# Expert places by half tiles of 64 tokens: 12 whole tiles, 7 pairs of halves and one half in place of 23 whole tiles

## The reference

```
logits = xf @ gate_w + gate_b                    # 2048 x 8
pb = softmax(logits);  top 1 of 8 experts per token
for each expert e:                               # scan
    h = gelu(xf @ w1[e] + b1[e])                 # 256 -> 1024
    y = h @ w2[e] + b2[e]                        # 1024 -> 256
    acc = acc + weight[:, e] * y                 # weight is 0 for the experts not chosen
x = x + acc
```

## Time and profile before

| | us |
|---|---|
| median of 3 runs | 841.37 |
| the profiled execution, whole time | 840.62 |
| its span, first to last instruction | 838.8 |
| TensorE busy in the span | 770.2 (92%) |
| VectorE, ScalarE, GpSimd busy | 442.7, 255.5, 186.9 |
| last stage: first tile's first product starts at | 661.4 |
| last scatter issued at | 832.4 |

### The profile page before, as it was taken

How to read it: one execution, slowest core, us unless ns; L and a number is a source line. 1 busy time by engine, 2 the same in 40 slices (tenths; PEclk the granted TensorE clock), 3 DMA queues, 4 the chain that set the end, 5 groups by cost and what they waited for, 6 DMA issues and landing times.

```text
span 838.8 us, 11312 instructions
## 1 busy us (share of the span) xinstructions
PE 770.2 (92%) x4207; PEld 625.8 (75%) x4207; DVE 442.7 (53%) x845; ACT 255.5 (30%) x502; POOL 186.9 (22%) x180
## 2 busy tenths in 40 slices
PE   5998999998989999999999999889886599999996
PEld 4665676687878878887888787645565599999995
DVE  3564678988922953295339532787966311111111
ACT  1533314222211221122122212455642223333331
POOL 3012353533000200020002000455631222222221
PEclk9999999999999999999999999979997699999999
DMA  9962600005000000000000000090122767776640
GB/s 327 385 201 88 264 0 2 1 0 202 2 1 2 2 3 2 2 2 2 2 2 2 2 2 3 8 394 1 51 76 76 255 221 219 227 214 218 205 137 0
DMA packets 20524, 79.68 MB, mean 95 GB/s; under 512 B 3053, under 2 KB 12400, under 8 KB 15664
## 3 DMA queue, kind: packets, MB, share of 16 engines
q1 hardware_dynamic: 17504, 70.44, 24.5%
q0 software_dynamic: 2944, 8.13, 2.5%
HBM read 72.27 MB, written 18.74 MB: 109 GB/s over the span
## 4 chain that ended last, share of the span: by engine, by line
PE 73%; DVE 18%; issue 5%; ACT 3%; DMA 1%; POOL 0%; DVEq 0%; SPq 0%; ACTq 0%; POOLq 0%
PE ps L1133 28%; PE ps L1824 10%; PE ps L1836 9%; PE ps L550 4%; PE ps L501 3%; PE ps L487 2%; DVE f_ha_hi L1233 2%; DVE f_raw L1227 2%; PE ps L1271 2%; DVE head_max L1661 1%; PE ps L579 1%; DVE stats L282 1%; PE ps L1408 1%; DVE c_tok L1662 1%; PE ps L1420 1%
## 5 line engine op out<-in xcount | busy, mean ns | idle before, releaser
L1210 ACT ACTIVATE f_raw<-ps,cols 128x512 f32<-128x512 f32 x96 | 66.2, 690 | 250.2 <-PE ps L1133 218.6
L1133 PE MATMUL ps<-f_hb_hi,fh 128*128 128x512 f32 x256 | 101.2, 395 | 2.5 <-DVE inexact L335 2.5
L1133 PE MATMUL ps<-f_ha_hi,fh 128*128 128x512 f32 x256 | 100.0, 391 | 3.2 <-ACT f_raw L1210 3.2
L1133 PE MATMUL ps<-f_hb_lo,fh 128*128 128x512 f32 x256 | 100.6, 393 | 0.0
L1133 PE MATMUL ps<-f_ha_lo,fh 128*128 128x512 f32 x256 | 99.6, 389 | 0.0
L1824 PEld LDWEIGHTS ps<-xsT,ew 128*128 128x128 f32 x736 | 87.2, 195 | 2.8 <-DVE xsT L1951 1.7
L1824 PE MATMUL ps<-xsT,ew 128*128 128x128 f32 x736 | 87.7, 278 | 1.1 <-DVE xsT L1951 1.1
L1884 ACT ACTIVATE hT<-ps,ew 128x128 f32<-128x128 f32 x184 | 52.5, 369 | 105.6 <-PE ps L1824 105.6
L1836 PE MATMUL ps<-ew,hT 128*128 x368 | 83.1, 379 | 0.0
L1233 DVE CAST f_ha_hi<-f_raw 128x512 fp32r<-128x512 f32 x64 | 32.8, 512 | 89.4 <-ACT f_raw L1210 88.3
L1836 PEld LDWEIGHTS ps<-ew,hT 128*128 128x128 f32 x368 | 68.2, 190 | 8.4
(11 more groups left out here) (241 smaller groups left out, 1290.0 us busy)
## 6 DMA issues: line engine op xcount, KB each, us to landing
ew<-in_ew SPq DMA_DIRECT2D x23, 1028.0 KB, 5.9
fh<-fh_copy SPq DMA_DIRECT2D x2, 4096.0 KB, 15.0
ew<-in_ew SPq DMA_DIRECT2D x1, 8192.0 KB, 23.4
fw<-fw_copy SPq DMA_DIRECT2D x3, 1024.0 KB, 7.1
eb<-in_eb SPq DMA_DIRECT2D x23, 128.0 KB, 3.3
x_res<-in_x SPq DMA_DIRECT2D x4, 512.0 KB, 10.8
rows<-x_res SPq DMA_DIRECT2D x4, 512.0 KB, 3.0
rows<-xn_e SPq DMA_DIRECT2D x4, 512.0 KB, 3.1
```

The source lines that it names most:

```text
L1133: ins = nc.tensor.matmul(out, *((xk, wk) if swap else (wk, xk)), start=(k == 0 and part == 0), stop=(k == w.shape[1] - 1 and part == 1))
L1210: nc.scalar.activation(f_raw[:, m % 3, :], ps[:, ring_bank(n), :], ACT.Silu if m < KH else ACT.Gelu, scale=col(("w1_s", "h1_s", "h2_s")[m ...
```

## The change

Places are given out by halves of 64 instead of tiles of 128. Each expert gets as many whole tiles as its number of halves allows (`g_first_i[:, 0]`, an even number of halves) and at most one odd half (`g_first_i[:, 1]`). The program has 12 tiles that belong to one expert each, 7 tiles that are pairs of halves with an expert of its own for each half, and one half alone: 20 tiles. They are worked in the order 0 to 3 whole, then a pair and a whole one by turns, then the last whole one and the half (`ORDER`). Loads of first weights become 27 in place of 23, in a ring of 6 buffers in place of 4.

For a pair, `up` makes 32 calls with 64 moving columns, 16 for each expert, and the gelu is 16 instructions of 64 columns. `down` makes 16 calls: for each k one with the 64 places of the first expert, which writes partitions 0 to 63, and one for the second expert, which writes partitions 64 to 127 (two column tiles of the array). The second one's weights are copied beforehand by VectorE from `ew2` to `ew2_b` (`second_weights`). At the head of the stage the one-hot tables grow from 23 to 40 columns and some small instructions are added.

```
-MT = NT + E - 1
+MT = NT + E // 2
+MH = 2 * MT
+FULL = NT - E // 2
+ORDER = [0, 1, 2, 3]
+for _n in range(FULL, MT - 1):
+    ORDER += [_n, len(ORDER) - (_n - FULL)]
+ORDER += [FULL - 1, MT - 1]
+HALVES = [2 if FULL <= _n < MT - 1 else 1 for _n in ORDER]
...
+LOAD_RING = 6
+PAIRED = [t for t in range(MT) if HALVES[t] == 2]
...
         def up(t):
-                for h in range(2):
+                loads = [(FIRST_LOAD[t] + h) for h in range(HALVES[t])]
...
                     for q in range(4):
-                        for k in range(KD):
-                            at_ = k * HID + (4 * h + q) * P
-                            ins = nc.tensor.matmul(ps[:, 2 + 2 * (t % 2) + h, q * P:(q + 1) * P],
-                                                   ew1[u][:, at_:at_ + P], xsT[:, t % 2, k, :],
-                                                   start=(k == 0), stop=(k == KD - 1))
+                        for h, n in enumerate(loads):
+                            part = slice(0, P) if t in WHOLE else half_rows(h)
+                            for k in range(KD):
+                                at_ = k * HID + (4 * g + q) * P
+                                ins = nc.tensor.matmul(
+                                    ps[:, 2 + 2 * (t % 2) + g, q * P + part.start:q * P + part.stop],
+                                    ew1[n % LOAD_RING][:, at_:at_ + P], xsT[:, t % 2, k, part],
+                                    start=(k == 0), stop=(k == KD - 1))
...
         def down(t):
+                if t in PAIRED:
+                    pe.wait_ge(e_w2, PAIRED.index(t) + 1)
...
-                    ins = nc.tensor.matmul(ps[:, 6 + t % 2, 0:D], hT[:, t % 2, k, :],
+                    part = slice(0, P) if t in WHOLE else half_rows(0)
+                    ins = nc.tensor.matmul(ps[part, 6 + t % 2, 0:D], hT[:, t % 2, k, part],
                                            ew2[:, bass.ts(e, 1), k, :].rearrange("p a n -> p (a n)"),
                                            start=(k == 0), stop=(k == KH - 1))
+                    if HALVES[t] == 2:
+                        ins = nc.tensor.matmul(ps[half_rows(1), 6 + t % 2, 0:D], hT[:, t % 2, k, half_rows(1)],
+                                               ew2_b[:, PAIRED.index(t) % 2, k, :],
+                                               start=(k == 0), stop=(k == KH - 1))
...
+            def second_weights(i):
+                n = FIRST_LOAD[PAIRED[i]] + 1
+                e = dve.value_load(expert[0:1, n:n + 1], min_val=0, max_val=E - 1)
+                if i >= 2:
+                    dve.wait_ge(e_down_full, PAIRED[i - 2] + 1)
+                nc.vector.tensor_copy(ew2_b[:, i % 2].rearrange("p k n -> p (k n)"),
+                                      ew2[:, bass.ts(e, 1)].rearrange("p a k n -> p (a k n)")).then_inc(e_w2, 1)
```

More of the change, by code:

```diff
@@ L273, in build @@
         ld_ew, rows_stored = sem("ld_ew"), sem("rows_stored")
-        e_stored, e_gathered, e_w1, e_b2 = (
-            [sem(f"e_{n}{u}") for u in range(TURN)] for n in ("stored", "gathered", "w1", "b2"))
+        e_stored, e_gathered, e_b2 = ([sem(f"e_{n}{u}") for u in range(TURN)] for n in ("stored", "gathered", "b2"))
+        e_w1 = [sem(f"e_w1{r}") for r in range(LOAD_RING)]
+        e_w2 = sem("e_w2")
         def moments(order, i, chunks):
@@ L1757, in attn1_vector, with b2_loads, half_rows @@
             gate_logits(LAST)
+        def b2_loads(t):
+            return sum(HALVES[s] for s in range(t % TURN, t + 1, TURN))
+        def half_rows(h):
+            return slice(h * HS, (h + 1) * HS)
         def moe_sync(sp):
@@ L1763, in moe_sync @@
                 u = t % TURN
[L1764 to L1769, removed]
+                experts = []
+                for h in range(HALVES[t]):
+                    n = FIRST_LOAD[t] + h
+                    r = n % LOAD_RING
+                    e = sp.value_load(expert[0:1, n:n + 1], min_val=0, max_val=E - 1)
+                    experts.append(e)
+                    if n == 1:
+                        sp.wait_ge(e_gathered[0], 16)
+                    if n >= LOAD_RING:
+                        sp.wait_ge(e_h, 2 * (SLOT_OF[n - LOAD_RING] + 1))
+                    sp.dma_start(ew1[r][:], ew1_d[bass.ts(e, 1)].rearrange("a p n -> p (a n)")).then_inc(e_w1[r], 16)
                 if t >= TURN:
@@ L1773, in moe_sync @@
                     sp.wait_ge(rows_stored, 16 * 2 * B)
-                sp.dma_start(eb2[:, u, :], eb2_d[bass.ts(e, 1), :].broadcast_to([P, D])).then_inc(e_b2[u], 16)
+                for h, e in enumerate(experts):
+                    part = half_rows(h) if t not in WHOLE else slice(0, P)
+                    sp.dma_start(eb2[part, u, :], eb2_d[bass.ts(e, 1), :].broadcast_to([part.stop - part.start, D]))\
+                        .then_inc(e_b2[u], 16)
         def moe_gpsimd(pool):
@@ L1903, in moe_vector @@
[L1903 to L1906, removed]
-            ends, starts = g_first[0][:, E:2 * E], g_first[0][:, E - 1:2 * E - 1]
+            order.step(nc.vector.tensor_scalar(g_count[:], total, float(HS - 1), None, ALU.add))
@@ new lines, in moe_vector @@
+            order.step(nc.vector.tensor_reduce(g_sel[:], g_pick[:], AX.X, ALU.add))
+            order.mark(nc.vector.tensor_tensor(g_tile[:], g_sel[:, :, 2], g_hi[:], ALU.add))
+            order.step(nc.vector.tensor_tensor(g_odd[:], g_hi[:], g_sel[:, :, 0], ALU.is_ge))
+            order.step(nc.vector.tensor_tensor(g_odd[:], g_odd[:], g_sel[:, :, 1], ALU.mult))
+            order.step(nc.vector.tensor_tensor(g_tile[:], g_tile[:], g_odd[:], ALU.add))
+            half_no = con("half_no", MH).unsqueeze(1).broadcast_to([P, NT, MH])
@@ new lines, in moe_vector @@
+            order.step(nc.vector.tensor_reduce(g_eid[:], g_cmp2[:].rearrange("p l a e -> p l (a e)"), AX.X, ALU.add))
+            order.step(nc.vector.tensor_copy(g_eid_i[:], g_eid[:]))
+            nc.vector.tensor_scalar(expert[:], g_eid_i[:], E - 1, None, ALU.bitwise_and).then_inc(expert_ready, 1)
+            nc.vector.tensor_tensor(g_ex[:], g_e[:], spread(g_max[:]), ALU.subtract).then_inc(scalar_in, 1)
+            dve.wait_ge(slots_full, 1)
+            for h in range(2):
+                order.mark(nc.vector.tensor_copy(
+                    g_places[half_rows(h)], ps[half_rows(h), 6, 0:2 * MH].rearrange("p (a h m) -> p a h m", a=2, h=2)
+                    [:, :, h, :]))
```

180 lines of the change are left out of this document (108 added, 72 removed).

## The result

The changed kernel takes 848.11 us (median of four runs, 846.28 to 851.72) against 841.37: a ratio of 1.0096, 95% interval 1.0076 to 1.0116. It is slower by 6.7 us; 848.6 was predicted. The profiled execution took 851.72 us with a span of 848.8, the longest of the four, so its parts are compared one by one with those of before, and not its total.

The account below looks back on a forecast made before the run. TensorE's own stream was taken to bound the last stage, VectorE's chain its head: 840.62 + 4.4 (steady part) + 2.8 (head) = 847.8, plus 0.75 for the median, 848.6 us; range 844 to 860.

Parts of the forecast that it names:

- A pair's `up`: Last stage, TensorE: 64 matmuls of 64 columns, rate set by the weights' load at 111 ns, 7.10 us.
- A pair's `down`: Last stage, TensorE: 32 matmuls in two column halves running side by side, 0.114 us each, 3.65 us.
- The third rival: Column halves in a pair's down do not run side by side: 6.9 us there, 872 in all; chance 4%.
- A pair: Last stage, TensorE: up, transposes and down, 7.10 + 0.22 + 3.65 = 10.97 us, against 7.24 for a whole tile.
- The half tile: End of the last stage: the lone half takes 7.2 us on TensorE, as much as a whole tile.
- The steady sum: Last stage, TensorE: 12 whole tiles, seven pairs and the half take 170.9 us against 166.5, so +4.4 us.
- What lies beside it: Last stage: ScalarE's gelu, VectorE's copy of second weights (2.3 us a pair) and transfers stay hidden, adding nothing.
- The head: Start of the last stage: VectorE's added small instructions delay the first gather, which still ends last; +2.8 us.
- The clock: TensorE's clock: low at the stage's head, nothing added, ±1 us kept; granted 1.00 through the pairs.
- The first rival: TensorE's clock falls in a pair's up: 873 us, or 855 to 865 if only now and then; chance 14%.
- The total: Whole kernel: 848.6 us as median, 7.2 us or 0.9% slower.
- The second rival: Half the moving columns halve a pair's up to 3.6 us: 822.5 us in all, faster; chance 7%.

Follow-up runs that it names:

- exchanged operands: Changed kernel, but in a pair's up tokens are stationary and weights move, with a VectorE copy and 8 transposes added: 833.82 us, in a second round 832.60 us.
- the 128-column run: Changed kernel, but each expert of a pair gets all 128 tokens as moving columns in up, the first result overwritten: 848.99 us, ratio to before 1.0100.

## Why the prediction was right

Step by step, by its own terms.

- *A pair's `up`*: 64 x 0.111 = 7.10 us was taken from the two streams with 1 and 8 moving columns; it measured 7.09 in the first pair and 7.19 with the change back from the column halves in front of it. 8, 64 and 128 columns gave 0.105, 0.112 and 0.113 us. This step decided the sign, and the experiments show that the moving columns don't set the rate. That the load does is argued from there. A fixed cost of any matmul is excluded: a bfloat16 stream of the kernel before (L1846, 46 moving columns) took 0.86 / 16 = 54 ns for one, even at a granted clock of 0.50. But a fixed cost of each float32 load with its matmul is not: no run has float32 weights of fewer than 128 columns with few moving ones. Of the two rules of "TensorE: Matmul & The Clock Gate" that the Trainium skill has, the one in section LDWEIGHTS agrees with this trace (107 ns there for 128 columns, 105 to 113 here). The table in section "Back-to-back issue gap" is given there for single matmuls without their loads; each matmul here brings its own float32 weights, and the halving by the table did not come.
- *A pair's `down`*: 3.65 predicted, 3.60 measured in each pair; 7.05 when the halves are put into one. The third rival (no running side by side) is excluded.
- *A pair*: 10.97 predicted, 11.12 measured. The 0.15 is entering the column halves (0.09: 0.31 us from the transposes to `down` in place of 0.22) and leaving them (0.10 in the next `up`), less 0.05 for a cheaper `down`. The prediction took both changes as included in the rates of L1408 and L579; from the first start of L579 to the start of its follower only the leaving is.
- *The half tile*: predicted to cost a whole one. The end of the stage came 0.4 us cheaper: from the last `up` to the end of the span it is 848.8 − 830.34 = 18.5 us against 838.8 − 819.95 = 18.9.
- *The steady sum*: +4.4 predicted, +4.9 measured.
- *What lies beside it*: the copy, ScalarE and the transfers cost nothing, as argued; the copy's own time was 1.23 us, not 2.3 (the rate was read from instructions of another kind).
- *The head*: +2.8 predicted, +2.83 measured (2.82 to 2.84 in each of the nine traces with that head). That the two agree is in part luck, since the reason was wrong: I had the gathered rows end last by 1.1 us, and it was the weights. `token_in` came 3.1 us later, not 2.8 (657.85 − 648.79 = 9.06 against 652.73 − 646.80 = 5.93). The weights came 4.87 us later, not 3.8 (from `g_count` to the last row of `weight` 664.77 − 648.79 = 15.98 against 657.91 − 646.80 = 11.11). The 0.3 of `token_in` is part of that, and 0.66 is the gate weights' product, 1.78 us in place of 1.12, at the low clock both times (0.50 in the windows): 111 ns for a matmul of 120 columns, 70 ns for one of 69. I had taken its rate as unchanged. Of the 4.87 us the old wait for the gather took up 2.04 (the transposes started 2.32 us after that last row of `weight`, now 0.28), which leaves 2.83. And the first gather must have landed sooner after its issue than before: 6.3 us as before would have brought the rows at 658.92 + 6.3 = 665.2, after the transposes started (665.05). In the last trace of the exchanged operands it took 5.9 us and landed 0.1 us ahead of the weights; why it took less is not shown.
- *The clock*: level 1.00 through all pairs of the changed kernel. The first rival did not occur, though it was worth its 14%: with 8 columns it did.
- *The total*: the traces' parts make 8.0 us, the two pairs of medians 6.7 and 9.2, the prediction 7.2. The close agreement is better than the parts deserve: the pairs were 0.15 us each too cheap (1.0 in all), the end of the stage 0.4 too dear.

The second rival (half the columns, half the time, 822.5 us) is excluded by the 111 ns of the 64-column stream and by the 128-column run. That 20 whole tiles take 821.5 us shows what the change would have had to reach.

## What to carry to other kernels

Before splitting a matmul's moving operand to save padding, look in the trace for a stream with the same weights and few columns: where its rate equals that of the full one, the moving columns do not bound it, and the product of a split tile costs double. What can be split without loss is the stationary side, in column halves that run side by side; exchange the operands so that the short dimension lies there, even at the price of transposes. And a reordering that adds columns to one-hot tables at the head of a stage has its price in small VectorE instructions on the way to the first product, and in TensorE's products with these tables; the 2.0 us of slack beside the gather hid only part of it.

## What was not expected of the hardware

- TensorE's granted clock fell from 1.00 to 0.50 within an unbroken stream of 64 weight loads with 8-column matmuls, at 100% busy in the profile. With 64 columns in the same stream it stayed at 1.00. A busy share of 100% is thus no sign that the clock stays up.
- A VectorE copy of 128x2048 float32 within the on-chip memory took 1.23 us, 0.6 ns an element, where the small instructions of the head take 1.04 ns. The Trainium skill has this in "VectorE: DVE Perf Modes", section "The perf-mode tier table (the rule you actually need)": a float32 copy that stays in that memory runs at twice the base rate, 1227 ns for 2048 elements. The trace agrees, and I would have had the price from there.
- A float32 transpose on TensorE is one matmul of 110 ns in the trace (8 in 713.75 − 712.87 = 0.88 us); the other float32 calls of this stage are two.
- Two traced executions of one kernel (exchanged operands) differ by 5.4 us, of which 5.2 lie ahead of the stage that was changed, and the granted clock there differs between them (0.83 and 0.94 from 540 to 570 us). A time alone would not have told this from an effect of the change.
